# Second stage of a fused image kernel: the front in two parts, the Newton steps beside the next image's front

## The reference, cut to what matters

```python
t = t + _L2_attn_ref(_ln_t(t), ...)   # landmark attention
t = t + _L2_ffn_ref(_ln_t(t), ...)    # 8 experts, top 2

# landmark attention: every 64th token is a landmark (16), 8 heads
kernel_1 = softmax(q @ k_lm.T * scale)
kernel_2 = softmax(q_lm @ k_lm.T * scale)
kernel_3 = softmax(q_lm @ k.T * scale)
z = kernel_2.T / fro**2
for _ in range(6):                    # Newton steps
    z = 2.0 * z - z @ kernel_2 @ z
out = kernel_1 @ (z @ (kernel_3 @ v))
```

## Time and profile before

| | us |
|---|---|
| median of 3 runs | 5303.67 (5300.96 to 5309.0) |
| the profiled execution | 5304.72 |
| its span, first to last instruction | 5302.9 |
| second stage, front 0 to the last step with a front | 2137.0 to 3571.4 |
| granted PE clock, mean of the span | 0.959 |

### The profile page before, as it was taken

One profiled execution on the slowest core, in us unless ns is written; L12 is line 12 of the kernel. 1 busy time (PEld: TensorE's weight loads), 2 busy tenths in 40 slices (PEclk: granted clock), 3 DMA queues, 4 the chain that ended last, 5 costly groups with the idle time before them and its releaser, 6 DMA issues.

```text
span 5302.9 us, 81731 instructions
## 1 busy us (share of the span) xinstructions
PE 4738.9 (89%) x25633; PEld 2629.4 (50%) x25633; DVE 3577.1 (67%) x7651; ACT 2996.8 (57%) x5516; POOL 1023.8 (19%) x1349
## 2 busy tenths in 40 slices
PE   6999999999999969588888888888999999999999
PEld 1222222222222223367777878777655555555554
DVE  6788888888888636556565655655577667667765
ACT  2666667676676724145555555557655554554552
POOL 2222223222232212023333333333100000000000
PEclk7999999999999989689999999999999999999999
DMA  2622223322233112235454554544211111111112
GB/s 61 166 78 69 73 66 98 84 66 77 66 92 83 49 31 28 68 111 169 135 169 138 154 152 145 162 132 134 64 49 52 45 48 51 47 47 51 49 45 76
DMA packets 396856, 461.35 MB, mean 87 GB/s; under 512 B 86136, under 2 KB 248144, under 8 KB 394320
## 3 DMA queue, kind: packets, MB, share of 16 engines
q1 hardware_dynamic: 362688, 409.11, 26.7%
q0 software_dynamic: 20576, 35.55, 2.4%
q10 hardware_dynamic: 13168, 11.48, 0.8%
HBM read 309.59 MB, written 129.84 MB: 83 GB/s over the span
## 4 chain that ended last, share of the span: by engine, by line
PE 34%; DVE 16%; issue 4%; DVEq 4%; ACT 2%; ACTq 0%; SPq 0%; DMA 0%
PE n_ps_f L2212 4%; PE n_ps_f L2205 4%; PE n_ps_xy L1860 4%; PE n_ps_h L1850 3%; PE n_ps_c L2252 3%; PE n_ps_h L2264 2%; PE n_ps_f L2199 2%; PE n_ps_f L1708 2%; DVEq L2084 1%; PE n_ps_xy L2268 1%; PE n_ps_f L1054 1%; DVE n_stats L1030 1%; PE n_ps_h L2268 1%; DVE n_xln L1042 1%; DVE n_down_weights L2083 1%
## 5 line engine op out<-in xcount | busy, mean ns | idle before, releaser
L664 ACT ACTIVATE a_probs<-ps_b 128x512 f32<-128x512 f32 x2048 | 1111.3, 595 | 558.7 <-PE ps_b L748 535.6
L496 DVE TENSOR_REDUCE a_negmax<-ps_a 128x1 f32<-128x1024 f32 x1024 | 1214.5, 1220 | 242.3 <-PE ps_a L696 213.0
L1663 ACT ACTIVATE n_hidden<-n_ps_h,n_b 128x128 f32<-128x128 f32 x1472 | 419.1, 373 | 346.9 <-PE n_ps_h L1850 346.1
L760 PE MATMUL ps_o<-a_probs,a_v_ones 128*32 128x512 f32 x4096 | 547.6, 607 | 0.5 <-ACT a_probs L664 0.5
L1860 PE MATMUL n_ps_xy<-n_down_weights,n_hidden 128*128 x2944 | 411.9, 284 | 79.2 <-ACT n_xy L1677 73.3
L696 PE MATMUL ps_a<-a_k_stack,a_q_stack 96*128 96x512 bf16 x1408 | 404.0, 394 | 58.5 <-DMA a_k_stack<-split_scratch 27.5
L748 PE MATMUL ps_b<-a_q_stack,a_k_stack 99*128 99x512 bf16 x1408 | 442.3, 386 | 14.8 <-ACT a_probs L664 11.9
L1860 PEld LDWEIGHTS n_ps_xy<-n_down_weights,n_hidden 128*128 128x128 f32 x2944 | 370.7, 196 | 117.3 <-issue 113.2
L2149 ACT ACTIVATE n_down_weights<-n_ps_h 128x512 f32<-128x512 f32 x288 | 172.2, 598 | 427.1 <-PE n_ps_h L2264 319.1
L1850 PE MATMUL n_ps_h<-n_xy,n_up_weights 128*128 128x128 f32 x2944 | 403.2, 281 | 3.2 <-issue 1.5
L1368 POOL DMA_INDIRECT rows_scratch<-n_xln,n_index_out x256 | 257.1, 1004 | 666.8 <-DVE n_index_out L1521 563.2
(11 more groups left out here) (349 smaller groups left out, 8154.3 us busy)
## 6 DMA issues: line engine op xcount, KB each, us to landing
n_up_weights<-in_L_ffn_W_dram SPq DMA_DIRECT2D x368, 256.0 KB
n_up_weights<-score_scratch SPq DMA_DIRECT2D x512, 128.0 KB, 2.9
split_scratch<-a_pieces SPq DMA_DIRECT2D x128, 256.0 KB
rows_scratch<-n_zero SPq DMA_DIRECT2D x16, 1472.0 KB, 9.6
outs_scratch<-n_xy SPq DMA_DIRECT2D x176, 128.0 KB
n_xg<-rows_scratch SPq DMA_DIRECT2D x80, 256.0 KB, 3.4
a_q_stack<-split_scratch SPq DMA_DIRECT2D x66, 256.0 KB, 5.0
a_k_stack<-split_scratch SPq DMA_DIRECT2D x66, 256.0 KB, 5.6
```

Of the source, the lines that this page charges most:

```text
L496: dve.tensor_reduce(negmax[:, b, t:t + 1], bank, axis=AX.X, op=ALU.max, negate=True).then_inc(ring_read, 1)
L664: act.activation(probs[:, m % PROBS, 512 * k:512 * k + 512], ps_b[:, k, :], ACT.Exp).then_inc(b_exp, 1)
L760: last = pe.matmul(ps_o[32 * j:32 * j + 32, 512 * k:512 * k + 512], v_ones[:, t, J * g + j, :], probs[:, (J * quad + j) % PROBS, 512 * k:5 ...
L1663: last = act.activation(hidden[:, j % 2, f, :], ps_h[j % 2][:, 128 * f:128 * f + 128], ACT.Gelu, bias=b1[:, bass.ds(e, 1), f:f + 1].rearra ...
```

## The change

`front` ends with kv. A new generator `back` takes the Newton steps, the two small products, the product with kernel_1 and the token sum, and runs one pipeline step later, beside the next image's front: PE in slots 1, 3, 5, ... 23 for Newton, 26, 28, 34 and 36 for the rest, DVE in the even slots 2 to 24, then 27, 29, 35 and 37. The list of a step is front of image i+3, back of i+2, choice of i+1, in that order within a slot. There is one more step before the experts begin, and the step of image 13 has a back and no front.

PSUM of the front becomes four banks of 512 columns: three (`banks`) that the front's products take in turn in halves, and one (`pn`) for `back`. The gate, the token turning, q, k, v, s1, the exp of kernel_1, its division and the turnings are all done in halves, each with its own semaphore counts (`filled`, `read`, `bank_free`). Token turning moves from slot 6 to 5 on PE, its copy from 7 to 6 on ACT; the turning of the normalised tokens from 13 to 12, q from 15 to 14, k from 16 to 15 on PE. s3 goes to slot 23, its maximum to 25, its exp to 26.

Buffers that two images now need are doubled (`tok_next`, `m2t`, `kv`), and kernel_1's turned copy has a tile of its own. The room comes from the third stage's gate, whose two comparison tiles (2048 columns each) now lie in a `tok_next` and that copy, with 1024 columns; `gate_choose_steps` therefore goes over the eight token tiles in two parts there. SP loads each image one step earlier in its list. The diff, cut:

```diff
 def gate_choose_steps(dve, t, E, K, eps, tie):
     p, rank, chosen = t["probs"], t["rank"], t["chosen"]
+    tiles = t["above"].shape[1] // E
     dve.tensor_reduce(t["total"][:, :], p[:, :, :], axis=AX.X, op=ALU.add)
+    for lo in range(0, NT, tiles):
...
+        dve.tensor_tensor(above, other, own, ALU.is_gt)
+        yield dve.tensor_tensor(same, other, own, ALU.is_equal)
+        dve.drain()
...
+        yield dve.tensor_tensor(flat, flat, tie..., ALU.mult)
+        dve.drain()
+        dve.tensor_tensor(t["above"][:, :, :], t["above"][:, :, :], t["same"][:, :, :], ALU.add)
+        dve.drain()
+        yield dve.tensor_reduce(rank[:, lo:lo + tiles, :], above, axis=AX.X, op=ALU.add)
+        dve.drain()
...
+        banks, pn = (pa[:, 0:512], pa[:, 512:1024], pb_[:, 0:512]), pb_[:, 512:1024]
+        BY_DVE, BY_ACT = "gate v s2 s1 norm kv".split(), "tok lnt q k s3 k1t e3t".split()
+        units = [(x, k) for x in "gate tok lnt q k v".split() for k in range(HALVES)] + [("s2", 0), ("s1", 0), ("s1", 1), ("s3", 0), ("s3", 1)]
+        units += [("norm", 0), ("k1t", 0), ("k1t", 1), ("e3t", 0), ("e3t", 1), ("kv", 0)]
+        bank_of = {unit: banks[n % 3] for n, unit in enumerate(units)}
+        def filled(i, x, k=0):
+            return S["front_ps"], i * len(units) + units.index((x, k)) + 1
+        def read(i, x, k=0):
+            kind, up = (BY_DVE, S["read_v"]) if x in BY_DVE else (BY_ACT, S["read_a"])
+            mine = [unit for unit in units if unit[0] in kind]
+            return up, i * len(mine) + mine.index((x, k)) + 1
+        def bank_free(i, x, k):
+            n = units.index((x, k))
+            return read(i, *units[n - 3]) if n >= 3 else read(i - 1, ...)
...
             side_by_side([front(0)])
-            side_by_side([front(1), choice(0)])
+            side_by_side([front(1), back(0)])
+            side_by_side([front(2), back(1), choice(0)])
             if begin:
                 begin()
-            experts(0, [front(2), choice(1)])
-            for i in range(1, B - 2):
-                experts(i, [front(i + 2), choice(i + 1)])
+            for i in range(B - 3):
+                experts(i, [front(i + 3), back(i + 2), choice(i + 1)])
+            experts(B - 3, [back(B - 1), choice(B - 2)])
             experts(B - 2, [choice(B - 1), dense_attention(0)])
...
-            for i in (1, 2):
+            for i in (1, 2, 3):
                 load_next(i)
...
             # DVE, front
                 yield 4
-                dve.scalar_tensor_tensor(u[:, :], pa[:, :], b3[:, :], u[:, :], ALU.add, ALU.mult)
+                for k in range(HALVES):
+                    dve.wait_ge(*filled(i, "gate", k))
+                    dve.scalar_tensor_tensor(u[:, half], bank_of["gate", k], b3[:, :], u[:, half], ALU.add, ALU.mult).then_inc(S["read_v"], 1)
+                    dve.drain()
+                    dve.tensor_tensor(u[:, half], u[:, half], x1[:, half], ALU.add).then_inc(S["x2_up"], 1)
                 yield 7
-                token_norm(dve, xln, tok_next, stats, mv, var, inv, tmp).then_inc(S["ln_up"], 1)
+                for n, last in enumerate(token_norm_steps(dve, xln, tok_nexts[i % 2], stats, mv, var, inv, tmp)):
+                    if n >= 4:
+                        last.then_inc(S["ln_up"], 1)
...
+            # DVE
+            def back(i):
+                yield 0
+                dve.tensor_scalar(z[:, :], m2t[:, :], fro[:, :], None, ALU.mult)
+                dve.tensor_scalar(zt[:, :], m2[:, :], fro[:, :], None, ALU.mult).then_inc(S["z0_up"], 1)
                 for it in range(NEWTON):
-                    yield 24 + 2 * it
+                    yield 2 + 4 * it
                     dve.drain()
                     dve.wait_ge(mz_ps, i * NEWTON + it + 1)
-                    dve.tensor_copy(mz[:, :], pa[:, 0:128]).then_inc(mz_up, 1)
-                    yield 25 + 2 * it
+                    dve.tensor_copy(mz[:, :], pn[:, 0:128]).then_inc(mz_up, 1)
+                    yield 4 + 4 * it
                     dve.wait_ge(znew_ps, i * NEWTON + it + 1)
...
             # ACT, front
-                yield 7
-                act.wait_ge(S["tok_ps"], i + 1)
+                yield 6
+                for k in range(HALVES):
+                    move(tok_nexts[i % 2][:, :, :].rearrange("p t c -> p (t c)"), "tok", k)
...
+                for k in range(HALVES):
+                    yield 22 + k
+                    act.wait_ge(S["d_up"], i * 3 + 2 + k)
+                    act.activation(k1[:, 4 * k:4 * k + 4, :], k1[:, 4 * k:4 * k + 4, :], ACT.Exp, scale=SCALE).then_inc(S["e_up"], 1)
...
+            # PE
+            def back(i):
                 for it in range(NEWTON):
-                    yield 24 + 2 * it
+                    yield 1 + 4 * it
                     if it == 0:
                         pe.wait_ge(S["z0_up"], i + 1)
                     else:
                         pe.wait_ge(z_up, i * NEWTON + it)
+                    pe.matmul(pn[:, 0:128], m2t[:, :], z[:, :], start=True, stop=True).then_inc(mz_ps, 1)
+                    yield 3 + 4 * it
                     pe.wait_ge(mz_up, i * NEWTON + it + 1)
+                    pe.matmul(pn[:, 128:256], zt[:, :], mz[:, :], start=True, stop=True)
+                    pe.matmul(pn[:, 256:384], mz[:, :], zt[:, :], start=True, stop=True).then_inc(znew_ps, 1)
```

More of the change, by code:

```diff
@@ L1605, in _ @@
             dense_attention, dense_choice, run_dense = dense["vector"](dve)
-            pipeline(dve, front, choice, experts, dense_attention, dense_choice, lambda: take_up(0))
+            pipeline(dve, (front, back), choice, experts, dense_attention, dense_choice, lambda: take_up(0))
             dve.wait_ge(y_ps, after(B - 1, LAST))
@@ new lines, in front @@
+                yield 26
+                act.wait_ge(S["max3_up"], i + 1)
+                act.activation(e3[:, :, :].rearrange("p t n -> p (t n)"), pa[:, :], ACT.Exp, scale=SCALE, bias=max3[:, :], accum_out=sum3[:, :]).then_inc(S["read_a"], 2)
+                yield 38
+                if i:
+                    act.wait_ge(S["attn_up"], i)
+                for k in range(HALVES):
+                    move(k1t, "k1t", k)
+                yield 40
+                for k in range(HALVES):
+                    move(e3t, "e3t", k)
@@ L1695, in _ @@
             dense_attention, dense_choice, run_dense = dense["scalar"](act)
[L1696 removed]
+            pipeline(act, (front, lambda i: iter(())), choice, experts, dense_attention, dense_choice, first_rows)
             act.wait_ge(y_ps, after(B - 1, LAST))
@@ new lines, in front @@
+                yield 5
+                for k in range(HALVES):
+                    bank, half = begin("tok", k)
+                    pe.wait_ge(S["x2_up"], i * HALVES + k + 1)
+                    for t in range(4):
+                        col = 512 * k + 128 * t
+                        last = pe.transpose(bank[:, 128 * t:128 * t + 128], u[:, col:col + 128], ident)
+                    last.then_inc(S["front_ps"], 1)
+                yield 12
+                turned("lnt", xln)
+                for n, x in enumerate("qk"):
+                    yield 14 + n
+                    for k in range(HALVES):
+                        bank, half = begin(x, k)
+                        pe.wait_ge(*read(i, "lnt", k))
+                        pe.matmul(bank, wqkv[:, C * n:C * n + C], xt[:, half], start=True, stop=True).then_inc(S["front_ps"], 1)
@@ new lines, in front @@
+                yield 17
+                for k in range(HALVES):
+                    bank, half = begin("v", k)
+                    for t in range(4):
+                        col = 512 * k + 128 * t
+                        last = pe.matmul(bank[:, 128 * t:128 * t + 128], xt[:, col:col + 128], wqkv[:, 2 * C:3 * C], start=True, stop=True)
+                    last.then_inc(S["front_ps"], 1)
+                yield 19
+                bank, _ = begin("s2")
+                pe.wait_ge(S["lm_up"], i + 1)
@@ L1785, in front @@
-                last.then_inc(S["attn_ps"], 1)
+                pe.wait_ge(*read(i, "k1t", 1))
+                for k in range(HALVES):
+                    yield 34 + 2 * k
+                    if k:
+                        pe.wait_ge(S["attn_half"], i + 1)
+                    for t in range(4):
+                        col = 512 * k + 128 * t
+                        last = pe.matmul(pn[:, 128 * t:128 * t + 128], k1t[:, col:col + 128], mixed_p[:, :], start=True, stop=True)
+                    last.then_inc(S["attn_ps"], 1)
@@ L1892, in _ @@
             dense_attention, dense_choice, run_dense = dense["tensor"](pe)
-            pipeline(pe, front, choice, experts, dense_attention, dense_choice, first_rows)
+            pipeline(pe, (front, back), choice, experts, dense_attention, dense_choice, first_rows)
             down(B - 1, LAST)
```

304 lines of the change are left out of this document (151 added, 153 removed).

## The result

The changed kernel takes 5406.43 us (median of 4 runs, 5400.02 to 5409.12); the kernel before takes 5304.09 beside it. The ratio is 1.019, 95% interval 1.0173 to 1.0208: **102 us slower, where I forecast 50**. The direction was right and the time lies in the range, but half of the loss was not in my sum.

| stretch | before, us | after, us | difference | forecast |
|---|---|---|---|---|
| up to the first expert step | 2292.3 | 2322.7 | +30.4 | +22 |
| 13 steps with front and choice | 1192.7 | 1259.0 | +66.3 | +51 |
| the fourteenth step | 89.1 | 68.7 | -20.4 | -27 |
| steps 15 and 16 | 196.3 | 195.0 | -1.3 | 0 |
| third stage | 1532.6 | 1558.3 | +25.7 | +4 |

What follows compares the result with a forecast made beforehand. PE's work (some 80 us) plus 10.9 us of waits bound each 91.6 us step. +51 for 13 steps, -5 for the extra pipeline step and +4 for the third stage, on 5304.7, gave 5354 us, range 5265 to 5410.

Steps and rivals of the forecast that it cites:

- Slot 9: PE's Newton product waits for DVE's update behind front's normalisation: 5.1 us a step.
- slot 3: PE's Newton product waits for DVE's copy behind choice's normalisation: 2.5 us, replacing 2.0 before the token turning.
- choice's second half: Slots 6 and 7: PE waits for ACT's late copy of choice's first half of turned tokens: 1.2 us a step.
- ACT's moves: PE's waits for ACT: 1.2 us stays at a step's beginning; two more table loads bring 3.5 (2 to 4).
- lock step: Newton, slots 1 to 24: PE can't pass an odd slot before DVE finishes the even one, across DVE's long pieces.
- With the clock's share left as it is: 13 steps: new waits 14.8 less old 10.9 give +3.9 us a step, +51, assuming an unchanged granted clock.
- the clock as a rival: Waits of 2.5, 5.1 and 3.5 each bring 3 us more at 1.2 GHz: 4.5 a step, 5412; chance 0.10.
- Part 5: Third stage's gate in two halves: DVE's counting sums about 0.3 us late for PE's count; +3 to +8, taken 4.
- Part 4: One more pipeline step: beginning +22 us, fourteenth step -27, net -5, held to within 10.
- Front 2, back 1 and choice 0: Last step before the experts: 13 us more for choice, 71 us; the beginning totals 174, +22.
- The fourteenth step: Loses its front: 16 us of PE work, the 5.1, 1.2 and most of 3.5; 91.2 to about 64, -27.
- The signs that I named: Newton waits 2 to 6 us twice a step, router after, eight table loads, no gate-sum wait, steps 95.5 and 64.

Runs made afterwards that it cites:

- The Newton runs: Changed kernel with the Newton steps laid around DVE's two normalisations: 5368.21 us; with the two small products behind them also given more room: 5307.53 us.
- e10_slot3: Changed kernel with Newton steps and small products moved, but step 0 and half of step 1 put back to slots 1 to 7: 5301.42 us.
- e5_fill_slot9: Changed kernel plus 40 thrown-away products of 128 columns in PE's wait in slot 9: 5385.26 us.
- e2_before_gate2: Kernel before with only the third stage's gate in two halves, on tiles of 1024 columns: 5318.51 us.
- e9_all_fill: Changed kernel with Newton and small products moved, later third-stage count, e2's exp in slot 22, plus 14 thrown-away products in slot 31: 5275.02 us.
- e12_all_slot3_fill: e11_all_slot3 plus 15 thrown-away products in slot 3 and 14 in slot 31: 5264.58 us.
- e11_all_slot3: e10_slot3 plus the third stage's count one tile later and the exp of e2 in slot 22: 5272.15 us.
- e1_count_later: Changed kernel with the third stage's count, its reading and the turning of the scores one tile later: 5378.64 us.

## Why the prediction was right about the waits and wrong about the size

**The waits: right, nearly term by term.** Slot 9 was 5.1 and is 5.0 (65.5 over 13); slot 3 was 2.5 and is 2.0 in twelve of the steps (24.1); choice's second half 1.2 and 1.2; q 1.0 and 0.7; kv 0.3 and 0.6. ACT's moves were 1.2 and 3.5 and are 5.4 together (70.0 over 13; in the step shown 1.22, 1.91 and 2.64): the loads press on slot 27 too. 14.8 in both, so +3.9 against the 10.9 before, 51 us; PE's idle time in the 13 steps rose by 49.8. The Newton runs show that it is lock step, and that it isn't a matter of Newton alone: the small product behind it waited 4 us a step too when its DVE copy stood behind the division. But not each such wait costs its length: slot 3's only takes the place of another (`e10_slot3`).

**"With the clock's share left as it is": this step failed.** PE's own work in the 13 steps took 16.5 us more (1064.7 for 1048.2, the same products); 51 and 16.5 are the 66.3 measured, but for 1. The 16.5 are a net figure: by the estimate above the clock costs 37 us more than before (90 for 53), 2.8 a step, and the products at equal clock 20 less, which I hadn't foreseen either. I had the clock as a rival with 0.10 and 4.5 us a step, from 9 us more at 1.2 GHz; measured are 6.8 more. It belongs in the sum with the waits, as the 21 us of `e5_fill_slot9` show. The size is uncertain: the same second stage of before took 1048.2 us of PE in one execution and 1029.1 in another (`e2_before_gate2`).

**Part 5, "I take 4": mis-sized, 25.7.** I looked at when the counting sums end and at PE's count, and found them 0.3 us late. But PE's count also waits for the attention sum of slot 28, and that now stands behind the 1.9 us of counting on DVE. It is the coupling that I described for the Newton steps, overlooked in the third stage. It was the largest miss: 22 of the 51 us.

**Part 4, "Net -5": +8.7.** Two terms were off. Front 2, back 1 and choice 0: I let the experts begin when the step's engines are through. They begin when image 0's rows are there. POOL issues its last scatter at

```profile
2311.75 0.96 POOL L1392 DMA_INDIRECT rows_scratch<-n_xln,n_index_out  x1 [0.30 <-issue]
```

and PE stands idle until the rows are back:

```profile
2316.91 0.69 PE L1926 MATMUL n_ps_xy<-c_ident,n_xg 128*128 128x128 f32 x2 [4.48 <-DMA n_xg<-rows_scratch]
```

before, that wait was 0.7. POOL's first scatter starts 55.3 us into the step (56.1 before), and from the step's beginning to this turning it is 79.5 us, 81.4 before: the step that carries choice did not get shorter for the experts, and I had counted nothing for POOL there. This is read from the two traces; no run tests it. The fourteenth step: I subtracted 5.1, 1.2 and 3.5 us of new waits from a step of before, which doesn't contain them (and these terms add up to 26 at most, not 27). PE's work fell by 18.2 us (16 forecast), its idle time only from 12.3 to 8.3, of which 2.6 wait for rows.

**The signs that I named** came: Newton's products wait 2 to 5 us behind a normalisation twice a step, router behind them, eight table loads. Three did not: the step is 96.8, not 95.5, the one of about 64 is 68.7, and the third stage's count waits. What stays open: why `e9_all_fill` gains nothing where `e12_all_slot3_fill` does, which these run-to-run spreads can't tell.

## What to carry to other kernels

When a chain between two in-order engines is stretched over a longer stretch of the program, look at each of its hand-overs for a long piece ahead of it on either engine, and lay the chain around these pieces; the free share of an engine (DVE was idle for 41% of a step of before) did not show these waits. Add to each new wait of PE what the lower clock behind it costs; where a wait can't be removed, products that are thrown away may be worth as much as a restructured pipeline (34 us here, for two edits; 31 for the change with all mends in `e11_all_slot3`). Price a small edit in another stage by the same rules as the main one, above all what it puts ahead of a piece that somebody waits for.

## What the runs showed of the hardware

That two waits of 1.2 and 1.5 us close together are followed by 3.4 to 10.2 us at 1.2 GHz in 8 of 13 steps of the kernel before, and that 21 products of 0.12 us in them (34.1 us in 13 steps) bring 2.9 us a step back. That the same products take about twice as long there: 31 fill 6.8 us at 0.50, 60 at 1.00.

That two executions of the same second stage can differ by some 20 us in this: `e2_before_gate2` has that of the kernel before, yet its 13 steps took 1173.2 us at a clock of 0.97 (68.3 us at 1.2 GHz), against 1192.7 at 0.96 (105.8). That of the change, with its 5 us wait in each step, came out the same in both executions that there are: 1259.0 here and 1259.1 in `e1_count_later`, each with 194.6 us at 1.2 GHz.
